# First 3x3 convolution: the sums for the norm taken from output operations and squares instead of bn_stats

## The reference

```python
# block 0
out = relu(bn(conv1x1(x, w1) + b1, g1, be1))      # 512 -> 128 channels
out = relu(bn(conv3x3(out, w2) + b2, g2, be2))    # 128 -> 128, the stage of this change
out = bn(conv1x1(out, w3) + b3, g3, be3)          # 128 -> 512
x = relu(x + softplus(residual_scale) * out)
# block 1
out = conv1x1(x, w1) + bias1b
out = conv3x3(out + bias2a, w2) + bias2b
out = conv1x1(out + bias3a, w3) + bias3b
x = relu(out * rscale + rbias + x)
# bn(v): (v - mean) / sqrt(var + 1e-5) * gamma + beta, mean and var per channel over 32 x 14 x 14 = 6272 values
```

## Time and profile before

| | |
|---|---|
| median of three runs | 307.45 us |
| lowest, highest run | 302.16, 308.34 us |
| profiled execution, its own time | 307.26 us |
| its span | 305.5 us |
| mean granted TensorE clock | 0.959 of full speed |
| TensorE matmuls, weight loads busy | 279.1 us (91%), 264.7 us (87%) |
| VectorE busy | 264.0 us (86%) |
| ScalarE busy | 199.3 us (65%) |
| GpSimd busy | 22.8 us (7%) |
| first 3x3 convolution, first to last product matmul | 55.1 to 109.7 us |
| second norm's scale and shift ready | 114.2 us |

### The profile page before, as it was taken

How to read it: one execution, slowest core, us unless ns; L and a number is a source line. 1 busy time by engine, 2 the same in 40 slices (tenths; PEclk the granted TensorE clock), 3 DMA queues, 4 the chain that set the end, 5 groups by cost and what they waited for, 6 DMA issues and landing times.

```text
span 305.5 us, 3976 instructions
## 1 busy us (share of the span) xinstructions
PE 279.1 (91%) x1528; PEld 264.7 (87%) x1528; DVE 264.0 (86%) x375; ACT 199.3 (65%) x244; POOL 22.8 (7%) x22
## 2 busy tenths in 40 slices
PE   5798999799899988979789799999999999999992
PEld 2698996799899958869689799999999999999991
DVE  2789997989999965878899989999999998898693
ACT  4778873667655418712998766487695876755664
POOL 0000000000000009990000000000000000000000
PEclk9789999799999997977999799999999999999999
DMA  6999705000000000000000000003105031315078
GB/s 206 425 424 425 317 0 182 2 0 2 0 0 2 0 0 1 2 0 0 2 0 0 0 3 0 2 1 158 55 0 210 2 166 44 134 79 210 2 312 319
DMA packets 6673, 28.17 MB, mean 92 GB/s; under 512 B 896, under 2 KB 3456, under 8 KB 5760
## 3 DMA queue, kind: packets, MB, share of 16 engines
q1 hardware_dynamic: 6368, 27.92, 22.9%
q10 hardware_dynamic: 288, 0.01, 0.1%
HBM read 15.09 MB, written 12.85 MB: 91 GB/s over the span
## 4 chain that ended last, share of the span: by engine, by line
PE 60%; DVE 23%; ACT 10%; issue 2%; DMA 2%; SPq 1%; ACTq 0%; DVEq 0%
PE ps L968 36%; PE ps L1003 20%; DVE vl L698 3%; DVE vf L682 3%; DVE stats L721 2%; DMA x<-x_dram 2%; ACT x L519 2%; DVE xl L820 2%; ACT x L474 2%; DVE y L708 2%; ACT xh L481 1%; PE ps L1053 1%; PE ps L1047 1%; DVE x L815 1%; DVE y L716 1%
## 5 line engine op out<-in xcount | busy, mean ns | idle before, releaser
L474 ACT ACTIVATE x<-x,shift 128x784 f32<-128x784 f32 x32 | 29.9, 946 | 14.6 <-DVE x L815 14.5
L1003 PE MATMUL ps<-vh,wu0h 128*128 128x364 f32 (+1 forms) x96 | 33.6, 350 | 3.8 <-DVE vl L698 1.9
L820 DVE TENSOR_TENSOR xl<-x,xh 128x784 fp32r<-128x784 f32 x32 | 29.8, 970 | 6.3 <-ACT xh L481 6.3
L815 DVE SCALAR_TENSOR_TENSOR x<-ps,scale,x 128x784 f32<-128x784 f32 x32 | 32.6, 1029 | 1.2 <-PE ps L968 1.1
L1003 PE MATMUL ps<-vh,wu0l 128*128 128x364 f32 (+1 forms) x96 | 33.0, 344 | 0.0
L1003 PE MATMUL ps<-vh,wu1h 128*128 128x364 f32 (+1 forms) x96 | 32.5, 339 | 0.0
L1003 PE MATMUL ps<-vl,wu1h 128*128 128x364 f32 (+1 forms) x96 | 32.4, 338 | 0.0
L1003 PE MATMUL ps<-vh,wu1l 128*128 128x364 f32 (+1 forms) x96 | 32.3, 336 | 0.0
L857 DVE SCALAR_TENSOR_TENSOR x<-ps,scal,x 128x784 f32<-128x784 f32 x31 | 31.4, 1026 | 0.0
L1003 PE MATMUL ps<-vl,wu0h 128*128 128x364 f32 (+1 forms) x96 | 31.3, 335 | 0.0
L615 DVE TENSOR_TENSOR xl<-x,xh 128x1568 fp32r<-128x1568 f32 x14 | 24.9, 1781 | 3.5 <-ACT xh L344 3.4
(11 more groups left out here) (174 smaller groups left out, 738.5 us busy)
## 6 DMA issues: line engine op xcount, KB each, us to landing
x<-x_dram SPq DMA_DIRECT2D x15, 784.0 KB, 8.0
out_dram<-x SPq DMA_DIRECT2D x6, 1568.0 KB, 5.2
out_dram<-x SPq DMA_DIRECT2D x7, 392.0 KB, 2.9
raw<-w_dram SPq DMA_DIRECT2D x1, 1088.0 KB, 5.3
x<-x_dram SPq DMA_DIRECT2D x4, 196.0 KB, 5.1
raw<-w_dram SPq DMA_DIRECT2D x1, 576.0 KB, 10.2
raw<-w_dram SPq DMA_DIRECT2D x2, 256.0 KB, 2.7
out_dram<-x SPq DMA_DIRECT2D x2, 196.0 KB, 3.4
```

The lines of the kernel that those rows point to most:

```text
L474: nc.scalar.activation(x_quad(q, c), x_quad(q, c), ACT.Relu, bias=shift3[:, c:c + 1]).then_inc(x1_ready, 1)
L815: nc.vector.scalar_tensor_tensor(x_quad(q, c), ps[:, bank:bank + 2, 0:N], scale3[:, c:c + 1], x_quad(q, c), ALU.mult, ALU.add).then_inc(s_ ...
L820: nc.vector.tensor_tensor(pair(xl[:, c, :]), x_quad(q, c), pair(xh[:, c, :]).bitcast(F32), ALU.subtract).then_inc(xl_ready, 1)
L1003: return nc.tensor.matmul(by_row(ps[:, bank, 0:N])[:, :, a:RW - b], wu[part][:, TILE[k] + dw, :], by_row(v[:, k, :])[:, :, b:RW - a], star ...
```

## The change

`y2_last` gives each of its two operations an accumulator output: the sum of the half that it writes goes into a column of `sum2s`. ScalarE squares each finished quad into a scratch tile with an accumulator output for the sum of squares (`square2`), one turn after the quad's last product; the last quad is squared in two halves (`square2_last`), the first of which waits only for the first output operation. `y2_stats` and this stage's bn_aggr go. At the end VectorE sums the 16 sums and the 9 sums of squares, forms mean, mean of squares less the squared mean, clamps at zero and adds epsilon. The first norm's bn_stats stay. The diff is whole:

```diff
--- before.py
+++ after.py
@@ -86,6 +86,8 @@
         raw3_at = raw1_at + 4 * (WT + 6) * P
         raw3 = place("raw3", [P, CT, P], F32, raw3_at)
         ident = place("ident", [P, P], F32, raw3_at + 4 * CT * P)
+        squares = place("squares", [P, NQ], F32, raw3_at + 4 * (CT + 3) * P)
+        assert raw3_at + 4 * (CT + 3) * P + 4 * NQ <= work_at + 56896
 
 
         at3 = [place(f"at3_{b}", [P, 4, 2 * P], F32R, work_at + b * 4 * 8 * P) for b in range(3)]
@@ -129,6 +131,8 @@
 
         par, scal = small("par", NPAR), small("scal", NSC)
         stats = small("stats", U, 6)
+        sum2s, square2s = small("sum2s", U), small("square2s", Q + 1)
+        total2, mean2 = small("total2", 2), small("mean2", 2)
         mv = small("mv", 2)
         scale1, shift1, scale2, shift2 = (small(n, 1) for n in ("scale1", "shift1", "scale2", "shift2"))
         scale3, shift3 = small("scale3", CT), small("shift3", CT)
@@ -167,7 +171,8 @@
         var_ready, std_ready, bn_ready, mean_ready = (sem(n) for n in ("var_ready", "std_ready", "bn_ready", "mean_ready"))
         a1_ready, v0_ready, v0h_ready, v0l_ready, conv2_done = (
             sem(n) for n in ("a1_ready", "v0_ready", "v0h_ready", "v0l_ready", "conv2_done"))
-        y2a_ready, y2b_ready, y2_ready = (sem(n) for n in ("y2a_ready", "y2b_ready", "y2_ready"))
+        y2a_ready, y2b_ready, y2e_ready, y2_ready, square_ready = (
+            sem(n) for n in ("y2a_ready", "y2b_ready", "y2e_ready", "y2_ready", "square_ready"))
         sp_ready, sp_exp, sp_log = sem("sp_ready"), sem("sp_exp"), sem("sp_log")
         a2_act, a2_pool, pool_relu, asum_ready = (sem(n) for n in ("a2_act", "a2_pool", "pool_relu", "asum_ready"))
         turned, th_ready, tl_ready, moments_done = (sem(n) for n in ("turned", "th_ready", "tl_ready", "moments_done"))
@@ -393,6 +398,19 @@
                 nc.scalar.activation(y[:, q, N:NQ], ps[:, bank, 0:N], ACT.Copy, scale=-1.0)
                 nc.scalar.activation(y[:, q, 0:N], ps[:, bank + 1, 0:N], ACT.Copy).then_inc(y2a_ready, 1)
 
+            def square2(q):
+
+                act.wait_ge(y2_ready, q + 1)
+                if q > 0:
+                    act.wait_ge(square_ready, q)
+                nc.scalar.activation(squares[:, :], y[:, q, :], ACT.Square, accum_out=square2s[:, q:q + 1]).then_inc(square_ready, 1)
+
+            def square2_last(k):
+                act.wait_ge(*((y2e_ready, Q) if k == 0 else (y2_ready, Q)))
+                act.wait_ge(square_ready, Q - 1)
+                part = slice(k * N, k * N + N)
+                nc.scalar.activation(squares[:, part], y[:, Q - 1, part], ACT.Square, accum_out=square2s[:, Q - 1 + k:Q + k]).then_inc(square_ready, 1)
+
             act.wait_ge(pad_ready, 2)
             normalise1(0)
             normalise1(1)
@@ -405,6 +423,8 @@
                 evacuate2(q)
                 if q + 2 < Q:
                     normalise1(q + 2)
+                if q > 0:
+                    square2(q - 1)
                 if q == 0:
                     act.wait_ge(sp_ready, 1)
                     nc.scalar.activation(sp[:, 1:2], sp[:, 0:1], ACT.Exp, scale=-1.0).then_inc(sp_exp, 1)
@@ -421,6 +441,8 @@
                     nc.scalar.activation(wd[0][:, :, :], raw1[:, CT + TAPS:WT, :], ACT.Copy).then_inc(wdh_ready, 1)
                 if q == 6:
                     nc.scalar.activation(wa1[0][:, :, :], raw1[:, 0:CT, :], ACT.Copy).then_inc(wah_ready, 1)
+            square2_last(0)
+            square2_last(1)
             square_root(2)
             act.wait_ge(bn_ready, 2)
             act.wait_ge(y2_ready, Q)
@@ -712,13 +734,10 @@
                 dve.wait_ge(conv2_done, 4 * q + 4)
                 dve.wait_ge(y2b_ready, q + 1)
                 m = ps[:, 4 * (q % 2) + 3, 0:N]
-                nc.vector.scalar_tensor_tensor(y[:, q, 0:N], m, 0.5, y[:, q, 0:N], ALU.mult, ALU.add)
-                nc.vector.scalar_tensor_tensor(y[:, q, N:NQ], m, -0.5, y[:, q, N:NQ], ALU.mult, ALU.add).then_inc(y2_ready, 1)
-
-            def y2_stats(q):
-                dve.wait_ge(y2_ready, q + 1)
-                for u in (2 * q, 2 * q + 1):
-                    nc.vector.bn_stats(stats[:, u, :], y_unit(u)).then_inc(stats_done, 1)
+                nc.vector.scalar_tensor_tensor(y[:, q, 0:N], m, 0.5, y[:, q, 0:N], ALU.mult, ALU.add,
+                                               accum_out=sum2s[:, 2 * q:2 * q + 1]).then_inc(y2e_ready, 1)
+                nc.vector.scalar_tensor_tensor(y[:, q, N:NQ], m, -0.5, y[:, q, N:NQ], ALU.mult, ALU.add,
+                                               accum_out=sum2s[:, 2 * q + 1:2 * q + 2]).then_inc(y2_ready, 1)
 
             dve.wait_ge(u0h_ready, 2)
             u0h_outer, u0l_outer = (wu0[i][:, 0:6, :].rearrange("p (a b) n -> p a (b n)", a=2) for i in range(2))
@@ -740,8 +759,6 @@
                 v0_low(q, 1)
                 if q + 1 < Q:
                     v0_sums(q + 1)
-                if q > 0:
-                    y2_stats(q - 1)
                 if q + 1 < Q:
                     v0_low(q + 1, 0)
                 y2_sum(q)
@@ -764,9 +781,16 @@
                     nc.vector.tensor_tensor(bias_t2[:, :], sc(BIAS2B), sc(BIAS3A), ALU.add)
                     chain(nc.vector.scalar_tensor_tensor(bias_y[:, :], sc(BIAS3B), sc(RSCALE), sc(RBIAS), ALU.mult, ALU.add))
             y2_last(Q - 1)
-            y2_stats(Q - 1)
-            dve.wait_ge(stats_done, 2 * U)
-            batch_norm(2, col(B2), half_g[:, 1:2], col(BE2), scale2[:, :], shift2[:, :])
+            dve.wait_ge(y2_ready, Q)
+            chain(nc.vector.reduce_sum(total2[:, 0:1], sum2s[:, :], AXIS.X))
+            chain(nc.vector.tensor_scalar(mean2[:, 0:1], total2[:, 0:1], 1.0 / COUNT, None, ALU.mult))
+            nc.vector.tensor_tensor(mean2[:, 1:2], mean2[:, 0:1], mean2[:, 0:1], ALU.mult)
+            nc.vector.scalar_tensor_tensor(mean_off[:, 0:1], mean2[:, 0:1], col(B2), col(B2), ALU.add, ALU.subtract).then_inc(mean_ready, 1)
+            dve.wait_ge(square_ready, Q + 1)
+            chain(nc.vector.reduce_sum(total2[:, 1:2], square2s[:, :], AXIS.X))
+            chain(nc.vector.scalar_tensor_tensor(var_eps[:, 0:1], total2[:, 1:2], 1.0 / COUNT, mean2[:, 1:2], ALU.mult, ALU.subtract))
+            nc.vector.tensor_scalar(var_eps[:, 0:1], var_eps[:, 0:1], 0.0, EPS, ALU.max, ALU.add).then_inc(var_ready, 1)
+            scale_shift(2, 1, half_g[:, 1:2], col(BE2), scale2[:, :], shift2[:, :])
 
 
             def turned_low(i):
```

## The result

The first timing gave a median of 306.16 us over 20 runs (305.27 to 307.93) against 306.51 for the kernel before (302.16 to 308.51), and a ratio of **1.0062** (95% interval 1.0037 to 1.0087). Read as it stands, the changed kernel is slower by 0.6%, beyond its interval and opposite to the small gain that was forecast. The ratio compares only the runs of each kernel within 1.5% of that kernel's own fastest: since one run of the kernel before fell to 302.16, this left out its ten runs above 306.7 (mean of the other ten 304.51) and none of the changed kernel's twenty (mean 306.40). 306.40 / 304.51 is the 1.0062. Over all 20 and 20 runs the means are 306.14 and 306.40.

What follows compares the result with a forecast made beforehand. The prediction took ScalarE's chain, meeting VectorE's at y2_sum, to set the turn and hide the statistics. Convolution -0.07 and tail -0.3 made -0.4 us, 307.0 us against a median of 307.45; range 302.5 to 309.0.

Steps and rivals of the forecast that it cites:

- What bounds the turn: First 3x3 convolution: the statistics lie in the shadow of ScalarE's chain, which meets VectorE's at y2_sum within 0.10 us; 0.74.
- the 0.5 to 0.9 us: Sign expected in the profile after: VectorE idle this long before y2_sum, released by ScalarE's evacuation.
- Part 1 (a): Statistics leave the turn: at the handover from ScalarE to VectorE, y2_sum comes 0.03 us earlier per turn.
- Part 1 (b): Statistics leave the turn: the low part TensorE waits for starts 0.88 us earlier, counted once, not per turn.
- Part 2: Output operations at the head of the turn: each accumulator read adds a = 0.08 us, bounds 0 to 0.20, paid in full.
- 12a: Cost of twelve accumulator reads on VectorE, ten in five turns and two more, at a = 0.08 us each.
- -0.07: Forecast move in us of the convolution's end: 12 x 0.08 - 0.88 - 5 x 0.03; bounds -1.3 and +1.5.
- Rival C: Output operations with accumulators cost more than they save: 308.7 us at a = 0.20, 312.7 at half rate; 0.13, half rate 0.03.
- Part 3: ScalarE's square of 784 columns per quad takes 0.95 us, in 2.57 us of idle time, and costs nothing in the path.
- D: On ScalarE, Square needs table loads of 1.28 us, one in the path before the last square root: 308.3 us; chance 0.04.
- Part 4: Tail after the last matmul: variance ready 2.60 us after the last first output operation instead of 2.92, gain 0.3 us.
- The sum: Whole kernel: -0.07 - 0.3 = -0.4 us, bounds -1.7 and +1.4; 307.0 us against the median, practically no change.

Runs made afterwards that it cites:

- e3: The kernel before, with ScalarE's evacuation of products 1 and 0 put ahead of the second high part, statistics kept; ratio 1.0109 by five runs.
- e6: The changed kernel with ScalarE's evacuation ahead of the second high part, run again for its trace; median 302.25 us, ratio 0.986.
- e10: The changed kernel with VectorE's second low part moved ahead of the two output operations; median 303.85 us, ratio 0.9986.
- e7: The kernel before with accumulator outputs on the two output operations, sums unused, bn_stats kept, no squares; ratio 1.0015.
- e2: The changed kernel, unchanged, timed again; median 307.02 us, ratio 1.0112, six runs.
- e9: The changed kernel, unchanged, measured a third time; median 306.01 us, ratio 0.9985.
- e5: The kernel before, unchanged, run once more for another trace; 306.45 us.
- e13: The kernel before with idle matmuls in three TensorE pauses (38 for 28, 32 for 22, ten new); median 303.31 us, ratio 0.9963.
- e14: The changed kernel with idle matmuls in three TensorE pauses (38 for 28, 32 for 22, ten new); median 303.12 us, ratio 0.9943.
- e4: The changed kernel with ScalarE's evacuation ahead of the second high part; median 301.7 us, ratio 0.9908; its trace fell on a disturbed execution of 1488 us.

## Why the prediction was right or wrong

- *What bounds the turn: right.* VectorE idle for 0.82 before y2_sum, released by ScalarE; e3 and e6 show both sides of it. The prediction had the 0.5 to 0.9 us.
- *Part 1 (a), 0.03 per turn at the handover: wrong by its whole size, 0.15 in five turns.* y2_sum still starts 0.10 after the evacuation. ScalarE's chain was the one that ended last before the change too; VectorE's own was 0.04 shorter (e3).
- *Part 1 (b), 0.88 us for the earlier first low part: the failed step.* It looked at one of TensorE's two waits in a turn. Products 2 and 3 wait for the second low part, which stands behind the output operations and ends 1.95 us into the turn; once TensorE is 0.87 ahead, it waits there: its wait in the last turn moved from 103.30 to 106.28. The stage's last distance shrank by 0.10 (5.48 to 5.38), and that is all that came of the 0.88. e10 takes that wait away and gets another 0.75.
- *Part 2, accumulators: a = 0.08 was too much.* The pair costs 0.02 to 0.03 per turn (after, e7), so 12a was 0.16, not 0.96. This error and the two before nearly cancel (0.16 - 0.10 against 0.96 - 0.88 - 0.15), so it is luck that -0.07 stood close to the measured +0.06. Rival C with its half rate falls. "Vector Engine (DVE) Microarchitecture Reference" of the Trainium skill ("Points that are easy to get wrong") states the halving for two SBUF sources that are not bf16. With one source in PSUM the rows show 0.57 us with and without accumulator; no run here has an accumulator with both sources in SBUF.
- *Part 3, the square: right that it is hidden,* 1.76 us left. At its pitch it is 0.84, not 0.95. D falls: the table loads are four before and after. The estimate started from an operation with a pointer operand; the square has none, and its 0.85 is that of the copies without one (0.86). "ScalarE: Activation LUTs" of the Trainium skill (section "What ACT_TABLE_LOAD costs") gives about 93 ns for each such operand; 1.04 with two, 0.95 with one and 0.86 with none agree.
- *Part 4, the tail: 0.69, not 0.3.* The half squares run at 0.53 instead of 0.61, the read lets the first start at 0.61 instead of 0.70, and scale_shift came 0.09 faster. That 0.09 lies between its last two operations (start to start 0.28 before, 0.19 after). e7, whose mean is made as before, has 0.20 there too, so it came with the accumulator outputs; why is open.
- *The sum: -0.4 forecast, -0.65 in the traces at equal clock, and the first ratio +0.6%.* In the traces the stage gave +0.06 for -0.07 and the tail -0.69 for -0.3. The runs confirm neither: over all runs of both kernels the means differ by +0.31 (-0.16 to +0.75), and only the kernels with filled pauses go the way of the traces (-0.38, -1.21 to +0.40). The ratio's sign came from which runs it left out, on top of groups of runs that go with the granted clock. The prediction saw the spread of 302 to 308 and only widened its range for it. It should have said that a ratio near 1 could come out on either side of it whatever the stage does.

What stays open: no trace was taken of a run below 303 us of either kernel. Their mean granted clock of 0.977 to 0.988 says that they have fewer falls, not none (an estimate: at 0.982, half clock for 3.6% of 300 us, 11 us, against some 28 us at 0.954), but where these lie wasn't seen. The mean alone does not fix the time: six runs of the changed kernel at 0.981 took 305.98 to 306.44. And the changed kernel had one run below 303 in 38, the kernel before 18 in 144. That may be chance. A rival was not tested: the shorter tail shortens TensorE's pause there from 2.2 to 1.5 us, and e2 and e9 (not the first trace) have no fall right behind it but a longer one of 10.2 us at 131 to 132. So the change may itself alter how the falls come and so give back what its stage gains.

## What to carry to other kernels

An engine that is never idle may still not be the bound: list for each operation in the turn what it waits for on every engine, and look how close the second to last to arrive is. When a producer is moved ahead, follow its consumer to its *next* wait in the same turn before counting the gain. And before a ratio of half a percent is believed, time the unchanged kernel against itself: here that alone gave 1.005, and the means of all runs told another story than the ratio.

## What the runs showed of the hardware

- A DVE_READ_ACCUMULATOR is recorded with 0.08 us and starts together with the next operation, which it moves by 0.015 us at most; ScalarE's read moves the next by 0.09 (98.03 to 98.12).
- The granted clock fell to 0.50 of full speed, 1.2 GHz, for 3.4 to 10.2 us. Between 50 and 200 us they began inside a TensorE pause of 0.7 to 2.2 us or up to 2.2 us behind its end, but the same pause brought a fall in one execution and none in another: the 1.9 us at 53 did before and did not in e5, the 1.85 us at 165 to 167 did in e13 and did not in e14. Idle matmuls in three pauses were worth 2.6 us to a kernel that was not otherwise changed.
- Three executions were far off, two at 676 us and one at 1488 (e4). In the last the span was 1486.3 us and TensorE was busy for 1481.4 of it with the same 1528 matmuls, each some four times as long (1.35 us against 0.34), at a recorded granted clock of 1.00.
